# Low parts of the attention values on GpSimd in place of VectorE

## The reference, cut to what matters

```python
qkv = jax.nn.silu(hidden_states @ qkv_w.T)
qkv = qkv.reshape(b, s, h, 3, d)
v = jnp.moveaxis(qkv[:, :, :, 2], 2, 1)
...
scores = jnp.einsum('bhnd,bhmd->bhnm', cq, ck) * diag_decay
intra = jnp.einsum('bhnm,bhmd->bhnd', scores, cv)
inter = jnp.einsum('bhnd,bhde->bhne', cq * q_decay, kv)
...
gate = jax.nn.sigmoid(hidden_states @ gate_w.T)
return gate * normed @ out_w.T
```

## Time and profile before

| | |
|---|---|
| median of three runs | 993.08 us |
| the profiled execution | 994.48 us |
| its span | 992.7 us |
| TensorE (PE) busy | 982.8 us, 99% |
| VectorE (DVE) busy | 799.5 us, 81% |
| ScalarE (ACT) busy | 727.6 us, 73% |
| GpSimd (POOL) busy | 458.3 us, 46% |
| chain that ended last | PE 92%, DVE 2%, ACT 2%, DMA 1%, POOL 1% |

### The profile page before, as it was taken

One profiled execution on the slowest core, in us unless ns is written; L12 is line 12 of the kernel. 1 busy time (PEld: TensorE's weight loads), 2 busy tenths in 40 slices (PEclk: granted clock), 3 DMA queues, 4 the chain that ended last, 5 costly groups with the idle time before them and its releaser, 6 DMA issues.

```text
span 992.7 us, 15943 instructions
## 1 busy us (share of the span) xinstructions
PE 982.8 (99%) x5569; PEld 862.8 (87%) x5569; DVE 799.5 (81%) x1058; ACT 727.6 (73%) x1261; POOL 458.3 (46%) x426
## 2 busy tenths in 40 slices
PE   9999999999999999999999999999999999999997
PEld 7888998889888898889988898888988899888896
DVE  6667887878867889679877788778886788889877
ACT  6678885788767885788857887577867888587653
POOL 1353464346544463434653465444635345531423
PEclk9999999999999999999999999999999999999999
DMA  6021211211121012212111111210122121110402
GB/s 212 29 64 36 75 37 57 58 44 52 51 65 51 30 52 72 65 35 75 35 58 58 44 52 51 65 51 30 52 71 64 33 78 35 59 52 22 160 12 86
DMA packets 52800, 57.79 MB, mean 58 GB/s; under 512 B 4336, under 2 KB 47728, under 8 KB 52720
## 3 DMA queue, kind: packets, MB, share of 16 engines
q1 hardware_dynamic: 52720, 56.77, 18.3%
HBM read 54.65 MB, written 2.10 MB: 57 GB/s over the span
## 4 chain that ended last, share of the span: by engine, by line
PE 92%; DVE 2%; ACT 2%; issue 1%; DMA 1%; POOL 1%; SPq 0%; POOLq 0%; ACTq 0%; DVEq 0%
PE ps L2032 24%; PE ps L2033 24%; PE ps L2034 23%; PE ps L2026 3%; PE ps L2028 3%; PE ps L2027 3%; PE ps L2129 2%; PE ps L2123 2%; PE ps L2125 2%; PE ps L2124 2%; PE ps L2143 1%; DMA stage<-stream 1%; DVE wl L1201 1%; PE ps L2127 1%; PE ps L2145 1%
## 5 line engine op out<-in xcount | busy, mean ns | idle before, releaser
L1903 POOL TENSOR_TENSOR stage<-stage 128x512 f32<-128x512 f32 x75 | 106.2, 1416 | 352.6 <-DMA stage<-stream 289.7
L2032 PE MATMUL ps<-xh,wh 128*128 128x512 f32 x658 | 260.4, 396 | 1.4 <-ACT stg L517 1.0
L2033 PE MATMUL ps<-xl,wh 128*128 128x512 f32 x658 | 257.1, 391 | 0.0
L2034 PE MATMUL ps<-xh,wl 128*128 128x512 f32 x658 | 256.2, 389 | 0.0
L1201 DVE TENSOR_TENSOR wl<-stage,wh 128x768 fp32r<-128x768 f32 (+3 forms) x183 | 202.6, 1123 | 23.2 <-ACT wh L471 22.1
L471 ACT ACTIVATE wh<-stage 128x768 fp32r<-128x768 f32 (+3 forms) x183 | 147.6, 834 | 12.8 <-POOL stage L1910 6.9
L2032 PEld LDWEIGHTS ps<-xh,wh 128*128 128x128 f32 x658 | 123.7, 188 | 26.7 <-ACT ps L471 2.1
L2034 PEld LDWEIGHTS ps<-xh,wl 128*128 128x128 f32 x658 | 123.6, 188 | 26.7
L2033 PEld LDWEIGHTS ps<-xl,wh 128*128 128x128 f32 x658 | 123.7, 188 | 21.8
L1946 POOL TENSOR_TENSOR sqacc<-sqacc,sq 128x512 f32<-128x512 f32 x64 | 90.6, 1416 | 108.8 <-ACT sq L635 108.8
L471 ACT ACTIVATE ps<-ps 128x512 f32<-128x512 f32 x150 | 87.4, 586 | 52.5 <-PE ps L2034 43.2
(11 more groups left out here) (224 smaller groups left out, 2322.2 us busy)
## 6 DMA issues: line engine op xcount, KB each, us to landing
stage<-stream SPq DMA_DIRECT2D x75, 384.0 KB, 3.4
stage<-stream SPq DMA_DIRECT2D x79, 128.0 KB, 2.1
dec<-decay SPq DMA_DIRECT2D x32, 192.0 KB, 2.5
stage<-stream SPq DMA_DIRECT2D x13, 256.0 KB, 3.2
acc<-xt SPq DMA_DIRECT2D x8, 256.0 KB, 5.9
v<-x SPq DMA_DIRECT2D x8, 256.0 KB, 6.1
out<-v SPq DMA_DIRECT2D x8, 256.0 KB, 2.1
y_home<-lora_router SPq DMA_DIRECT2D x1, 512.0 KB, 5.0
```

The source lines that it names most:

```text
L1903: nc.gpsimd.tensor_tensor(stage[:, s, 1:5:3, :], stage[:, s, 0:6:5, :], stage[:, s, 7:8, :].broadcast_to([P, 2, U]), ALU.add).then_inc(t_p ...
L2032: nc.tensor.matmul(dst, wt[0], mv_[0], start=start, stop=False, skip_group_check=True)
L2033: nc.tensor.matmul(dst, wt[0], mv_[1], start=False, stop=False, skip_group_check=True)
L2034: return nc.tensor.matmul(dst, wt[1], mv_[0], start=False, stop=stop, skip_group_check=True)
```

## The change

`values_lo` moves from VectorE's queue to GpSimd's for heads 1 to 28. It is there two operations of four token tiles each (128x512), with the same inputs and output and the same semaphores (`v_hi` before, `v_lo` after the second). Head 0 and the last three heads (29, 30, 31) stay on VectorE. In GpSimd's queue the places are: the first head of a group behind the sums of g01 and in front of the sums of qk1 (groups 1 to 7); the second head behind the sums of qk3 (groups 0 to 6); the third behind a sum of squares and in front of the next group's sums of va (groups 0 to 6); the fourth in the next group behind `y_sums(g, 0)` (groups 1 to 7).

```diff
@@ def qk0(g), VectorE
                 c12_add(n)
-                values_lo(h - 1)
                 scores_lo(h - 1, 0)
@@ def output(g), VectorE
                 out_add(g, "c12", 1)
-                values_lo(h)
                 out_add(g, "c21", 0)
@@ def qk1(g) and def qk2(g), VectorE
                 add_part(h, 1)
-                values_lo(h + 1)
                 c22_add(n)
@@ GpSimd
+            def values_lo(h):
+
+                pool.wait_ge(v_hi, h + 1)
+                for i in range(2):
+                    tiles = slice(4 * i, 4 * i + 4)
+                    last = nc.gpsimd.tensor_tensor(vl[:, tiles, :], v[:, tiles, tile(h % HG)], f32(vh[:, tiles, :]),
+                                                   ALU.subtract)
+                last.then_inc(v_lo, 1)
+
@@ GpSimd, the loop over groups
                     y_sums(g, 0)
+                    values_lo(h - 1)
                     add_squares(h - 2, 1)
...
                     sums(g, "g01")
+                    values_lo(h)
                 sums(g, "qk1")
...
                 sums(g, "qk3")
+                values_lo(h + 1)
                 add_squares(h, 1)
                 next_sums(g, "qk0")
                 add_squares(h + 1, 0)
+                values_lo(h + 2)
                 next_sums(g, "va")
```

## The result

The changed kernel takes 1000.08 us (median of 4 runs, 998.98 to 1001.73), the kernel before 993.38 us beside it. The ratio is 1.0062 (95% interval 1.0041 to 1.0083). Five more rounds beside other runs of the kernel before gave 1.0074 (1.0062 to 1.0087). So the change costs 6.7 to 7.3 us.

A forecast was written before the change was run, and what follows sets the result against it. TensorE was taken as the bound. To the profiled 994.48 us came +9.6 (Place A), +0.5 (Place B), -0.5 (old gaps): 1004.1; with runs' median 1.4 lower, the forecast was 1002.7 us, range 993.2 to 1009.

The forecast's parts named there:

- The bound: Whole kernel: TensorE, busy 982.8 of 992.7 us, bounds it; taking 34 us off VectorE gives back between 0 and 1.5 us.
- Place A: Group's first head, before qk1's sums: late sums block ScalarE's bank copy, delaying TensorE's product 6; 7 x 1.37 = 9.6 us.
- the collisions: VectorE's yl and two wl alternate with GpSimd's operations behind g01's sums, delaying qk1's sums until 625.68.
- the seventh place: Group 7, first head: same distance from high part to copy (8.54 us), so the same 1.37 us gap was counted.
- The load: Load of qk2 after the low part of qk1 B: 0.4 us early against the delayed TensorE, so no second gap.
- Place B: Group's third head, before va's sums: VectorE's delayed k subtraction holds up scores, 0.07 us in 7 groups, 0.5 in all.
- old gaps: TensorE's existing waits, longest 1.0 us in two places: 0.5 us was to come back.
- Places C and D: Second head, and last head handled in the next group: 2.5 us fits into GpSimd's idle 6.87 and 8.84 us; cost 0.
- The signs: Profile after: seven bank-product waits near 1 us, high part waiting over 2, 56 operations (mean near 1.7), VectorE falling under 39.
- The rule on the lock: VectorE instructions with two SBUF inputs and GpSimd ones reading SBUF exclude each other throughout; without this, no gap.

The follow-up runs named there:

- wait alone: Changed kernel with first heads of groups 1 to 7 back on VectorE, GpSimd keeping only the wait for the values' high part: 993.72 us, 0.9995 of the kernel before.
- half of every head: Changed kernel with the low part of all 28 heads split, tiles 0 to 3 on GpSimd, 4 to 7 on VectorE: 997.25 us, 1.0029 of the kernel before.
- three operations: Changed kernel with one more GpSimd subtraction, the first half again, for each group's first head: 1016.38 us, 1.0214 of the kernel before.

## Why the prediction was right, point by point

**The bound.** Right: TensorE at 99%, so that VectorE's freed time gives nothing. VectorE's 34 us less work even became 9 us more busy time.

**Place A, the mechanism.** Right in each link up to the gap, and each was tried by itself: the order in GpSimd's queue (moved: no loss), the work and not the wait (wait alone: no loss), the order in ScalarE's queue (copy ahead: no loss with the sums as late as before), the collision (write-only operations: the two engines run side by side). The first head alone brings the whole loss.

**Place A, the size.** The term was 7 x 1.37 = 9.6 us; it measured 6 x 0.84 = 5.0 us. Two things in it were off. Both made it too large.
First, the collisions. I let each hold the other engine for the distance between two of VectorE's starts (1.14 us for yl, 0.87 for the first wl, 1.06 left of the second after the 0.08). The waits that show are 0.98 in the pair (3.54 - 2.56), 0.71 in the first sum (2.00 - 1.29) and 0.86 in the second (1.60 - 0.74). They are 0.16 to 0.20 shorter each, 0.52 together. The sums ended 9.12 us after the high part's start; I had 9.57.
Second, the seventh place. I took the equal distance of the two ScalarE instructions in group 7 for an equal cost, and did not look at what TensorE does between product 5 and product 6 there: attention products of 1.12 us, which hide it. The distance is not quite the same in the five groups between either: in group 4 it is 8.70 us (500.37 to 509.07), and there the gap is the smallest, 0.67.

**What the sum left out.** The first head alone costs 6.8 us, the six gaps are 5.0. The rest is found by laying each of TensorE's 5569 products in the profile after beside the same one before. Across the six places, from the last product ahead of the gap to 4 us behind it, TensorE falls behind by 1.02, 0.86, 1.04, 0.83, 1.01 and 1.11 us, 5.9 together. That is the gaps and some 0.15 us each of restart: the first product behind a gap is 0.33 us from the second (629.46 to 629.79) where the stream has 0.23. Another 0.9 us comes around one more gap, of 0.56 us, at 764.46 in group 6. Together this is 6.8. In the run with the first head alone it is 5.9 and 0.9 again (the later gap is at 765.89 there).

**The load, which was taken to be early enough.** This later gap is place A once more, by a way that the prediction had ruled out ("so no second gap follows from the load"). The view of the chain that ended last, 735 to 766, leads back from it:

```profile
748.15 2.30 DVE wl L1201
...
750.84 4.71 DMA stage<-stream
...
755.62 1.60 POOL stage L1899
...
761.13 1.59 POOL sqacc L1951
...
764.03 0.59 ACT q L517
```

The low part of qk1 B stands behind the late high parts. It starts at 748.15 where it was at 742.71, and takes 2.30 us where it took 2.14. It frees the staging half, so the load is issued at 750.84 where it was at 745.24 before, 5.60 us later; TensorE itself is 5.03 later there. Behind the load come the sums, a sum of squares, q and the product that waits. In group 5 the load is late as well (633.04 against 628.71, 4.33 us, with TensorE 3.83 late): 0.5 us late where the prediction had 0.4 early. It opens a gap only in group 6. With ScalarE's copy ahead of the high part the load of group 6 is issued 0.98 us earlier than before, with TensorE 1.08 earlier, and there is no such gap. No run delays the load alone, so this path is read from the traces and not shown by an experiment of its own.

**How near the total came, and why.** The forecast was 9.3 to 9.6 us, the change cost 6.7 to 7.3. Part of the nearness is luck: place A was put too high by 4.6 us of gaps, while restarts (0.9) and the later gap (0.9) were not in the sum. The 0.5 us for place B and the 0.5 for the old gaps did not come either, and had cancelled in the sum.

**Place B.** The 0.5 us did not show: the longest gaps before the scores that are new in the change are 0.16 and 0.14 us (at 652.16 and 654.97), and the run with the first head back on VectorE is level with the kernel before. But half of every head showed that the room is as small as was said: the second k subtraction ends 0.58 us before the scores in the kernel before (554.92 and 555.50) and 0.11 before them in that run (556.49 and 556.60), so the room is an estimated 0.5.

**Places C and D, old gaps.** C and D cost nothing, as taken: with the first head back on VectorE the time is that of before. Of the old gaps 0.5 us was to come back. In the changed kernel it did not: both are still there, 0.80 us at 62.39 and 0.56 at 412.93. The run with the first head behind the sums of qk1 is 0.1% faster than before, and the gap of 0.56 us at 410.79 in the kernel before is not in its trace.

**The signs.** The new entry came with six waits of 0.52 to 0.81 us at place A, not seven of 1 us. ScalarE's high part of qk1 A waits 6.1 to 6.4 us in each group, and the 56 operations have a median of 1.30 us and a mean of 1.57, as said. VectorE's busy time did not fall at all.

**The rule on the lock.** By SBUF — State Buffer of the Trainium skill (section Who interferes with whom) a VectorE instruction with two SBUF inputs contends with a GpSimd instruction that reads SBUF, and not with one that only writes it. The case agrees in both halves: with a reading GpSimd operation yl takes 1.82 us, with a writing one 1.22.

**The versions that beat both.** With the first head behind the sums of qk1 (0.9989, 0.9980 to 0.9999), or with half of it on VectorE (0.9989, 0.9980 to 0.9998), the kernel is 0.1% faster than before, at the edge of what can be told.

## What to carry to other kernels

When work moves to a less busy engine, its busy share says little; look at what stands behind the new instruction in that engine's queue, and behind whoever waits for that in the next queue, until an instruction of the bounding engine comes up with less room than the delay. Then read the same stretch once for each repetition of the pattern: the seventh group looked like the other six on two engines and not on the third. If the delay only just exceeds the room, half of the work or the next place in the queue can make the whole cost vanish, as both did here.

## What the runs showed of the hardware that had not been expected

TensorE's granted clock fell from 1.00 to 0.50 behind five of six gaps of 3.4 to 3.6 us and behind five of six gaps of 2.0 to 2.3 us, in a stream that was full up to them, and behind none of the six of 0.7 to 1.0 us. It did not fall behind each: of two gaps of 3.47 and 3.49 us the one at 403.87 was followed by it, the one at 646.37 was not. With three operations the fall accounts for the way from 1009 to 1016 us, by an estimate from the rows: behind each of the five gaps some eight products lie 0.43 us apart in place of 0.23, 8 x 0.2 x 5 = 8 us.

By one pair of rows, an engine that waits for the other is let in a little before the other's recorded end: the first sum of qk1 waited 0.71 us inside itself beside a VectorE instruction of which 0.86 us were left by its record (623.54 to 624.40), 0.15 less. No run was made for this.
